# Transformer layer with a mixture of experts on one core: the last norm's small arithmetic goes from GpSimd to VectorE, three of its additions from VectorE to GpSimd

## The reference, cut to what matters

```python
def _layernorm(x, axis=-1, eps=1e-05):
    m = jnp.mean(x, axis=axis, keepdims=True)
    v = jnp.var(x, axis=axis, keepdims=True)
    return (x - m) / jnp.sqrt(v + eps)
...
# x: (8, 256, 256), 2048 tokens of 256 numbers
x = x + _layernorm(attention(_layernorm(x)))      # 16 query heads on 4 key heads, rope, causal softmax
x = x + _layernorm(ffn(_layernorm(x)))
# ffn: a shared expert (hidden 352) times a sigmoid gate, plus 2 of 8 routed experts (hidden 176) per token
```

## Time and profile before

| | |
|---|---|
| Time, three runs | 679.06, 680.37, 681.21 us; median 680.37 |
| The profiled execution | 683.07 us, its span (first to last instruction) 681.0 us, mean granted TensorE clock 0.989 of full speed |
| Busy share of the span | PE 93%, DVE 83%, ACT 83%, POOL 81% |
| Indirect DMAs issued by GpSimd | 71 |

### The profile page before, as it was taken

One profiled execution on the slowest core, in us unless ns is written; L12 is line 12 of the kernel. 1 busy time (PEld: TensorE's weight loads), 2 busy tenths in 40 slices (PEclk: granted clock), 3 DMA queues, 4 the chain that ended last, 5 costly groups with the idle time before them and its releaser, 6 DMA issues.

```text
span 681.0 us, 15537 instructions
## 1 busy us (share of the span) xinstructions
PE 631.6 (93%) x4430; PEld 581.0 (85%) x4430; DVE 567.2 (83%) x1925; ACT 564.5 (83%) x2175; POOL 552.6 (81%) x590
## 2 busy tenths in 40 slices
PE   3668999999999999999999999999799999999993
PEld 2557899999999999999999999899688888999981
DVE  6899999998989889888888889999978854555576
ACT  5779999999989999998999999999888535666643
POOL 5799889999999999999999998989866424566654
PEclk9789999999999999999999999999999999999998
DMA  8001113999530000000000000000436124444263
GB/s 336 15 1 33 30 73 118 334 334 276 3 47 1 1 2 2 1 1 2 1 2 1 2 1 2 1 1 25 142 116 203 55 81 116 123 131 119 70 256 124
DMA packets 50978, 54.20 MB, mean 80 GB/s; under 512 B 19824, under 2 KB 42608, under 8 KB 50768
## 3 DMA queue, kind: packets, MB, share of 16 engines
q1 hardware_dynamic: 47488, 43.84, 22.3%
q0 software_dynamic: 3408, 9.38, 3.8%
HBM read 23.76 MB, written 29.51 MB: 78 GB/s over the span
## 4 chain that ended last, share of the span: by engine, by line
POOL 52%; PE 25%; ACT 10%; DVE 6%; issue 4%; DMA 1%; another core or an unknown queue 0%; ACTq 0%; SPq 0%; DVEq 0%; POOLq 0%
POOL ropes L2030 11%; POOL ropes L2020 11%; POOL ropes L2023 9%; POOL rs L2008 9%; PE pQ L459 2%; PE pQ L461 2%; PE pQ L460 2%; POOL hrow L2044 2%; ACT ropes L980 2%; ACT P L995 2%; POOL osb L2051 2%; PE pO L459 2%; POOL rs L2006 2%; POOL lr L2008 1%; PE pO L460 1%
## 5 line engine op out<-in xcount | busy, mean ns | idle before, releaser
L459 PE MATMUL pQ<-W 128*128 128x512 f32 (+2 forms) x334 | 119.3, 357 | 9.6 <-DVE W L1389 5.2
L995 ACT ACTIVATE P<-P,nmx 128x128 f32<-128x128 f32 (+1 forms) x256 | 119.9, 500 | 0.0
L460 PE MATMUL pQ<-W 128*128 128x512 f32 (+2 forms) x334 | 114.4, 342 | 0.0
L461 PE MATMUL pQ<-W 128*128 128x512 f32 (+2 forms) x334 | 113.8, 341 | 0.0
L1003 ACT ACTIVATE P<-P,rinv 128x128 f32<-128x128 f32 (+1 forms) x256 | 107.0, 490 | 1.8 <-DVE rinv L1462 1.6
L2020 POOL TENSOR_TENSOR ropes<-ropes 128x640 f32<-128x640 f32 x63 | 99.2, 1575 | 6.7 <-DVE ropes L1435 6.7
L2030 POOL TENSOR_TENSOR ropes<-ropes 128x640 f32<-128x640 f32 x63 | 100.1, 1589 | 4.9
L980 ACT ACTIVATE ropes<-pQ 128x128 f32<-128x128 f32 x320 | 89.3, 308 | 13.6 <-POOL ropes L2030 7.6
L459 PE MATMUL pO<-W 128*128 128x256 f32 (+1 forms) x323 | 95.1, 295 | 5.4 <-DVE W L1471 3.9
L1466 DVE TENSOR_TENSOR W<-pP,W 128x384 fp32r<-128x384 f32 x128 | 70.2, 548 | 27.6 <-ACT W L1008 27.3
L460 PE MATMUL pO<-W 128*128 128x256 f32 (+1 forms) x323 | 91.5, 283 | 0.0
(11 more groups left out here) (268 smaller groups left out, 2205.7 us busy)
## 6 DMA issues: line engine op xcount, KB each, us to landing
xs<-stage SPq DMA_DIRECT2D x1, 17550.0 KB, 58.4
stage<-xs SPq DMA_DIRECT2D x39, 130.0 KB
ropes<-in_ew SPq DMA_DIRECT2D x8, 608.0 KB
stage<-in_wqkv SPq DMA_DIRECT2D x3, 768.0 KB, 9.1
stage<-ys SPq DMA_DIRECT2D x4, 512.0 KB, 6.3
ropes<-ys SPq DMA_DIRECT2D x4, 512.0 KB, 7.4
out<-X SPq DMA_DIRECT2D x7, 256.0 KB, 2.0
X<-in_wo SPq DMA_DIRECT2D x1, 1536.0 KB, 13.1
```

What stands on the lines that cost most here:

```text
L459: e.matmul(out, lh, rh, start=start, stop=False, skip_group_check=True)
L460: e.matmul(out, lh, rl, start=False, stop=False, skip_group_check=True)
L461: return e.matmul(out, ll, rh, start=False, stop=stop, skip_group_check=True)
L995: a = e.activation(P[:, z, span(t)], P[:, z, span(t)], ACT.Exp, bias=nmx[:, z, t:t + 1], scale=-1.0, accum_out=sums[:, z, t:t + 1])
```

## The change

VectorE now makes variance plus eps (`last_var`) right behind the statistics, and negative mean times root in one instruction (`last_nb`) behind the power. GpSimd's `last_root` is the power alone. The additions to X of pairs 1, 3 and 5 (`POOLADD`) are GpSimd's, behind the powers, so that three of VectorE's seven 512-wide additions are gone from its list. Those that are left stand at other places. The transfers out keep their order and wait on the semaphore of the engine that made the addition.

```diff
+POOLADD = (1, 3, 5)
...
             for p in range(NPAIR - 1):
-                e.wait_ge(s_fres, p + 1)
+                if p in POOLADD:
+                    e.wait_ge(s_ysum, PPE + POOLADD.index(p) + 1)
+                else:
+                    e.wait_ge(s_fres, p // 2 + 1)
...
+            def last_var(p, n):
+                z = slice(p % 4, p % 4 + n)
+                if p >= 4:
+                    e.wait_ge(s_fapp, p + n - 4)
+                else:
+                    e.wait_ge(s_h2row, NT)
+                e.wait_ge(s_aggr2, NB + p + n)
+                e.tensor_scalar(lr2[:, z, :], mv2[:, z, :, 1], 1.0, EPS, ALU.mult, ALU.add).then_inc(s_var2, 1)
+
+            def last_nb(p, n):
+                z = slice(p % 4, p % 4 + n)
+                e.wait_ge(s_lr2, NB + root_of(p) + 1)
+                e.scalar_tensor_tensor(nb2[:, z, :], mv2[:, z, :, 0], -1.0, lr2[:, z, :], ALU.mult,
+                                       ALU.mult).then_inc(s_nb2, 1)
...
                 if q in PAIR:
                     if PAIR[q] < PPE:
                         last_sum(PAIR[q])
+                    if PAIR[q] == 4:
+                        last_nb(2, 2)
                     last_stats(PAIR[q])
+                    if PAIR[q] >= 6:
+                        last_var(PAIR[q], 1)
+                    elif PAIR[q] % 2 == 1:
+                        last_var(PAIR[q] - 1, 2)
...
-                p = PAIR.get(q - 2, 0)
-                if 0 < p < 6 and p % 2 == 1:
-                    last_add(p - 1)
-                    last_add(p)
+                p = PAIR.get(q, 0)
+                if p == 2:
+                    last_nb(0, 2)
+                elif p == 3:
+                    last_add(0)
                 elif p == 6:
-                    last_add(p)
+                    last_add(2)
+                    last_nb(4, 2)
                 elif p == 7:
-                    last_scale(p)
+                    last_nb(6, 1)
+                if PAIR.get(q - 1, 0) == 7:
+                    last_add(4)
+                    last_scale(7)
+                    last_add(6)
                     for t in range(2):
-                        last_add_tile(p, t)
+                        last_add_tile(7, t)
...
             def last_root(p, n):
...
-                e.wait_ge(s_aggr2, NB + p + n)
-                e.tensor_scalar(lr2[:, z, :], mv2[:, z, :, 1], 1.0, EPS, ALU.mult, ALU.add).then_inc(s_var2, 1)
-                if p < NPAIR - 1:
-                    e.tensor_scalar(nb2[:, z, :], mv2[:, z, :, 0], -1.0, None, ALU.mult)
-                e.wait_ge(s_var2, k + 1)
+                e.wait_ge(s_var2, NB + root_of(p) + 1)
                 e.tensor_tensor(lr2[:, z, :], lr2[:, z, :], half[:, 0:2 * n].rearrange("p (a b) -> p a b", a=n),
                                 ALU.pow).then_inc(s_lr2, 1)
-                if p < NPAIR - 1:
-                    e.wait_ge(s_lr2, k + 1)
-                    e.tensor_tensor(nb2[:, z, :], nb2[:, z, :], lr2[:, z, :], ALU.mult).then_inc(s_nb2, 1)
+
+            def last_add(p):
+                e.wait_ge(s_fapp, p + 1)
+                e.tensor_tensor(X[:, 2 * p:2 * p + 2, :], X[:, 2 * p:2 * p + 2, :], yl[p][:, :, 0:HID],
+                                ALU.add).then_inc(s_ysum, 1)
...
+                if p == 3:
+                    last_add(1)
+                elif p == 6:
+                    last_add(3)
+                elif p == 7:
+                    last_add(5)
```

More of the change, by code:

```diff
@@ L447, in _ @@
             for p in range(NPAIR - 1):
-                e.wait_ge(s_fres, p + 1)
+                if p in POOLADD:
+                    e.wait_ge(s_ysum, PPE + POOLADD.index(p) + 1)
+                else:
+                    e.wait_ge(s_fres, p // 2 + 1)
                 e.dma_start(out_d[:, 2 * p:2 * p + 2, :], X[:, 2 * p:2 * p + 2, :]).then_inc(s_out, 16)
             for m in (NT - 2, NT - 1):
-                e.wait_ge(s_fres, m - NT + NPAIR + 2)
+                e.wait_ge(s_fres, m - NT + 2 + NPAIR - len(POOLADD))
                 e.dma_start(out_d[:, m:m + 1, :], X[:, m:m + 1, :]).then_inc(s_out, 16)
@@ L1749, in last_scale @@
                                         lr2[:, p % 4, t:t + 1], ALU.subtract, ALU.mult)
-                a.then_inc(s_fapp, 1)
+                a.then_inc(s_fsum, 1)
             def last_add_tile(p, t):
-                e.wait_ge(s_fapp, p + 1)
+                e.wait_ge(s_fsum, PPE + 1)
                 e.tensor_tensor(X[:, 2 * p + t, :], X[:, 2 * p + t, :], yl[p][:, t, 0:HID],
@@ L2075, in last_root @@
             def last_root(p, n):
[L2076 to L2080, removed]
-                z = slice(p % 4, p % 4 + n)
-                e.wait_ge(s_aggr2, NB + p + n)
-                e.tensor_scalar(lr2[:, z, :], mv2[:, z, :, 1], 1.0, EPS, ALU.mult, ALU.add).then_inc(s_var2, 1)
-                if p < NPAIR - 1:
-                    e.tensor_scalar(nb2[:, z, :], mv2[:, z, :, 0], -1.0, None, ALU.mult)
-                e.wait_ge(s_var2, k + 1)
+                z = slice(p % 4, p % 4 + n)
+                e.wait_ge(s_var2, NB + root_of(p) + 1)
                 e.tensor_tensor(lr2[:, z, :], lr2[:, z, :], half[:, 0:2 * n].rearrange("p (a b) -> p a b", a=n),
                                 ALU.pow).then_inc(s_lr2, 1)
-                if p < NPAIR - 1:
-                    e.wait_ge(s_lr2, k + 1)
-                    e.tensor_tensor(nb2[:, z, :], nb2[:, z, :], lr2[:, z, :], ALU.mult).then_inc(s_nb2, 1)
+            def last_add(p):
+                e.wait_ge(s_fapp, p + 1)
+                e.tensor_tensor(X[:, 2 * p:2 * p + 2, :], X[:, 2 * p:2 * p + 2, :], yl[p][:, :, 0:HID],
+                                ALU.add).then_inc(s_ysum, 1)
             def row_tokens(a, b):
```

## The result

| | kernel before | changed kernel |
|---|---|---|
| Time, median of 7 runs each | 680.61 us (679.06 to 683.65) | 683.23 us (681.46 to 685.4) |
| The profiled execution | 683.07 us, span 681.0 | 682.12 us, span 680.0 |
| Mean granted TensorE clock in it | 0.989 of full speed | 0.985 |

The changed kernel is **slower: the ratio is 1.0039, 95% interval 1.0023 to 1.0055**, some 2.7 us with 1.1 on either side. The two profiled executions say the opposite (682.12 against 683.07), because executions differ long before the touched stretch begins: pair 1's statistics end at 659.65 in one and at 656.39 in the other. So I count from a point just ahead of it, the end of pair 1's statistics (the second of the aggregates that the earlier trace rows begin with), and call it the **anchor**: 659.65 before, 656.14 + 0.25 = 656.39 after.

What follows compares the result with a forecast made beforehand. TensorE is busiest, but the end was taken to follow GpSimd's last instruction through its 5.9 us drain. That instruction comes 1.51 us later, so +1.5 us on the median 680.37 gives 681.9 us; range 679.9 to 683.4.

Steps and rivals of the forecast that it cites:

- The likeliest case: Last 22 us: small variances are held, `nb` of pairs 2 and 3 goes ahead of addition 1; +1.5 us, chance 0.45.
- rival 4: `nb` of pairs 2 and 3 loses to GpSimd's addition 1 and is held: +1.2 us more, 683.1 us; chance 0.17.
- the sum: Step-by-step delays over the last 22 us, ending with GpSimd's last instruction 1.51 us later: +1.5 us.
- The end follows GpSimd's last instruction, 5.9 behind it: At the end, GpSimd's drain costs 5.9 us behind its last instruction, so the end moves one for one with it.
- The first variance is held, `u_lo(14)` is late and TensorE waits: GpSimd's sum of pair 4's halves holds variances of pairs 0 and 1; `u_lo(14)` is 1.00 us late, TensorE waits.
- rival 3: Small variances with columns lying apart aren't held and take 0.17 us each: +0.2 us, 680.6 us; chance 0.15.
- `nb` of pairs 2 and 3 takes 0.17: On VectorE, between sum and statistics of pair 4: it waits for the power, then runs unheld in 0.17 us.
- The last power and addition 5: GpSimd's end: last power 0.56 us behind addition 4, at 675.06; addition 5 then ends the list at 676.41.
- The skill's rule at sum 2: By the shared-port rule VectorE's sum 2 would wait some 0.3 us for the first power: 682.0 in place of 681.9.
- A count: Work moved: GpSimd loses two or three small instructions per root and gains three times 1.28 us.
- The chance of slower, 0.30: Chance given to the whole kernel being slower by more than some 0.3%, 2.0 us.

Runs made afterwards that it cites:

- experiment 1: Kernel before plus three GpSimd additions, whose result nobody reads, behind its last instruction; ratio 1.0058 against the kernel before.
- experiment 2: Kernel before plus one GpSimd drain behind the last of its 71 indirect DMAs; ratio 0.9984 against the kernel before.
- experiment 6: Changed kernel with the variances of pairs 0 and 1 moved behind `u_lo(14)` and the product for U tile 15; ratio 1.0024 against the kernel before.
- Experiment 3: Changed kernel, only that GpSimd's addition 1 also waits until `nb` of pairs 2 and 3 is made; ratio 1.0015 against the kernel before.
- 9: Changed kernel plus one GpSimd drain behind the scatters, ahead of the first selection; ratio 0.9996 against the kernel before.

## Why the prediction was right or wrong

The prediction was 681.9 us, slower by 0.2%; measured was slower by 0.39%, inside the range and near its upper end. The likeliest case was not the one that came, rival 4 was: the number lies in the range because the range took rival 4 in, and the sum itself gave little more than half of the lateness. By the prediction's own steps, in us behind the anchor:

| step | before | predicted | measured |
|---|---|---|---|
| `u_lo(14)` begins | -0.08 | 0.92 | 0.88 |
| power of 2 and 3 ends | 7.65 | 7.81 | 7.78 |
| `nb` of 2 and 3 takes | | 0.17 | 1.16 |
| stats of pair 4 begin | 6.80 | 7.94 | 8.96 |
| stats of pair 5 end | 8.99 | 10.13 | 11.13 |
| power of 4 and 5 ends | 11.66 | 11.46 | 12.50 |
| stats of pair 7 end | 12.87 | 13.22 | 14.27 |
| last power ends | 15.25 | 15.41 | 16.29 |
| last GpSimd instruction ends | 15.25 | 16.76 | 17.53 |
| last VectorE instruction ends | 17.32 | 18.05 | 18.74 |

- **The end follows GpSimd's last instruction, 5.9 behind it**: right, in the changed kernel's trace (5.90) and by experiments 1 and 2. That the 5.9 is a fixed price was wrong in a way that the sum didn't need: it grows with the indirect DMAs since the last drain.
- **The first variance is held, `u_lo(14)` is late and TensorE waits**: right (`u_lo(14)` is 0.96 late for 1.00; TensorE's wait grew from 0.35 to 1.31, and `u_lo(15)` begins 3.74 behind the anchor for the predicted 3.76, before 2.76). This rules out rival 3: small instructions whose columns lie apart are held as well. By experiment 6 it is worth some 0.65 at the end.
- **`nb` of pairs 2 and 3 takes 0.17**: this is the step that failed. I set VectorE 0.04 behind the power's end and GpSimd 0.08 behind it. In the trace the power ends at 662.78 + 1.38 = 664.16, the addition starts at 664.13 and `nb` at 664.26. GpSimd's addition had waited for nothing of the power and was there first, by 0.13; VectorE had a semaphore to wait for and came 0.10 behind. Both figures were wrong, and by these rows either alone would have lost the race, VectorE's by only 0.02. The 0.08 was read from GpSimd's product, which waits for the power; the addition doesn't. The 0.04 is too small wherever a small instruction of VectorE waits: the variances, too, start 0.10 behind the aggregates. Experiment 3, where the addition waits, has `nb` again 0.10 behind the power, and gains 0.95. It is the kernel of my likeliest case, and there the forecast fits: GpSimd's last instruction 16.6 behind the anchor for the predicted 16.76, ratio 1.0015 for 1.0022.
- **The last power and addition 5**: the mechanism was right. The variance of pair 7 ends with addition 3, addition 4 goes first, and the power ends 0.56 behind it. The lateness shrinks from 1.05 at pair 7's statistics to 0.77 at the end because additions 3 and 5 each begin 0.1 earlier behind a power than I had them: the same few hundredths that lost the race give back a little here.
- **The skill's rule at sum 2.** In the changed kernel's timeline sum 2 starts at 658.16, inside the first power (657.43 to 658.47), and takes its usual 0.68. The Trainium skill (SBUF — State Buffer, Who interferes with whom) would have it held; for the power the trace disagrees again, while for GpSimd's 512-wide addition 1 it agrees: `nb` of pairs 2 and 3, with both inputs in SBUF, was held until it ended. The two variances that were held have one SBUF input, of which this sentence of the skill doesn't speak.
- **A count.** The prediction says that GpSimd loses two or three small instructions per root. The root of pair 7 loses one; nothing in the sum hangs on it.
- **The size.** With `nb` held, rival 4 had 683.1, +2.7 at the end; measured is 2.3 in the traces and 2.7 with 1.1 on either side in the times. The chance of slower, 0.30, was too low: the race alone decided it, and I gave it 0.17 on a figure of 0.04 that no row showed for VectorE.

## What to carry to other kernels

Before work is moved to another engine, look at the barrier at the end: here one list reported 1.7 us behind all the others, and what was added to it counted in full (experiment 1), while VectorE had slack. If that list is GpSimd's and it has issued indirect DMAs, a drain in an earlier gap of its list makes the last one shorter, here 3.26 us in place of 5.90. When two engines both follow one instruction and one's long instruction can hold the other's short one, don't count on the short one to go first: here, in the three executions with this race (the changed kernel, 6 and 9), the engine whose list the instruction stands in won it each time. So give the long instruction the semaphore of the short one, or put the short one where the other engine is idle.

## What the runs showed of the hardware that I had not expected

- GpSimd's drain costs 0.065 us without indirect DMAs behind the last drain, 3.26 with 39 and 5.90 with 71: 0.082 us for each, although the transfers had landed long before (in the kernel before, the last packet of these DMAs ended at 648.4, over 26 us ahead of GpSimd's last instruction).
- GpSimd's additions, which wait for nothing of the power ahead of them, start 0.02 to 0.03 us ahead of its recorded end. Not every such instruction does: in the kernel before L2085 waits for nothing either and starts 0.08 behind L2083. VectorE's `nb` starts 0.10 behind the end of the power that it waits for, but its scale of pair 7 only 0.03 behind (672.71, the power's end being 672.68); why they differ stays open.
- The prediction had this as its likeliest case, but no row before showed it: a `tensor_scalar` of 2 or 4 columns that lie apart is held by a GpSimd instruction with two SBUF inputs as one with columns side by side is: 0.68 to 0.86 us in the changed kernel and 1.29 in 9, in place of 0.17.
